# A two-layer Mamba, attention and quantised-FFN kernel: every engine's order rewritten, and 162 products of the identity added on TensorE

## The chip, the core and the metric

The kernel runs on one core of a Trainium2 chip. The metric is the device time of one execution in microseconds (us), lower is better. Before the change it is 393.94 us, the median of three runs (392.65 to 394.93).

TensorE (PE in the profile) multiplies, VectorE (DVE), ScalarE (ACT) and GpSimd (POOL) do the elementwise work, and the SyncE queue (SP) issues most transfers. Each engine runs its own list of instructions in order; between engines there are only semaphores.

## The reference, cut to what matters

Sixteen sequences of 128 tokens (`x`) pass through three blocks, all in float32 (the FFN's weights are rounded to -1, 0, 1 and held as bf16):

```python
x = emb[input_ids]                                    # 16 x 128 x 192
for i in range(2):                                    # two Mamba layers
    xr, res = jnp.split(_rmsnorm(x, norm_w[i]) @ in_proj_w[i], 2, axis=-1)   # 2 x 384 columns
    xr = silu(conv4(xr) + conv_b)                     # causal, 4 taps, by channel
    dt, Bm, Cm = jnp.split(xr @ x_proj_w, [12, 28], axis=-1)
    delta = softplus(dt @ dt_proj_w + dt_proj_b)
    y = selective_scan(xr, delta, A, Bm, Cm, D)       # 16 states by channel
    x = x + y * silu(res) @ out_proj_w
h = x + attention(_layernorm(x))                      # 12 heads of 16; weights relu(1 + s + s*s/2), normalised
out = h + ffn(_layernorm(h))                          # rmsnorm, 8-bit rounding, 192 -> 2 x 512 -> 192
```

## The kernel before, in words

**Tiling.** The Mamba part works on chunks `j` = 0 to 7: layer `j // 4`, group `j % 4` of four sequences (512 columns: `GT`). The 384 channels are `CI` = 3 blocks `c` of 128 partitions. The attention and the FFN work on groups `g` of four sequences and on single sequences `s` = 0 to 15.

**One chunk.** `square_sums`, `raise_squares`, `root_inverse_in` and `scale` normalise; TensorE turns the rows (`turn_in`, line 972, transposes of 128x128), ScalarE takes them out of PSUM (`take_xt`), `project_in` and `project_rest` (lines 983, 989, 991) multiply by the input weights; `first_tap` (ACT) and nine `convolve` (DVE, line 2239) make the convolution; `silu_input`, `silu_gate_in` the activations; `project_x`, `take_xp` and `project_steps` (line 1005) lead to the steps; `magnitude`, `exponential`, `one_plus`, `error` (line 2231), `logarithm`, `rest` (POOL) and `delta` (line 2248) are the softplus. `spread_b` and `spread_cg` (lines 1010 to 1018) spread B and C over the partitions. `input_times_b` (2263), `scan_first` (2269), `memoryless_states` (2277), `skip` (2282), `times_c` (2288) and on POOL `add_first` (1856) and `gate` (1850) make the gated output, `project_out` (1065) projects it in two halves, and `add_h` (2335) adds it to `h`.

**The other states.** State 0 is scanned; for the other 15 a flag (`count_short`, `raise_flag`) tells whether they decay within one step. `states_pe`, `states_dve`, `states_act` load that flag and branch; with these inputs the branch around the loops is taken in all eight chunks.

**Attention and FFN.** `variances`, `root_inverse`, `normalise` (2360) and `turn_x` (1074) start the attention of a group; `project_qk`, `project_v`, then by sequence `scores` (1115), `square_scores` (ACT, 480), `values` (1127), `turn_sums` (1135 and 1138), `divide`, `turn_attention`, `project`. `scores(s)` waits until ScalarE has squared all of `s - 1`. The FFN of a sequence: `turn_input`, two `project_up` (1167), `silu_gate`, `hidden` (2439), `gain` (POOL, 1890), `square_hidden`, `hidden_root`, `hidden_step`, `round_hidden` (2453), `turn_hidden` (1174), `take_hidden` (534), `project_down` (1181), `add_ffn` (2459), and the store of the sequence.

**What sets the order.** Each engine's program is a written-out list of such calls, laid out beforehand by a planner with costs of its own. PSUM has eight banks of 512 columns; the tables `T_BANKS` to `UP_BANKS` give each product its bank, and bare `pe.wait_ge(...)` lines between the calls of TensorE's list wait until the bank's last reader is through. The lists of the four engines must fit each other: whatever stands at the head of a list and waits holds up all behind it.

**`keep_clock`** (line 965) is defined in the kernel before and called nowhere in it: `n` products of the 128x128 float32 identity with itself into bank `b`, with no semaphore; nothing reads the result.

## Time and profile before

| | |
|---|---|
| median of three runs | 393.94 us (392.65 to 394.93) |
| the profiled execution's own time | 396.22 us |
| its span, first to last instruction | 394.2 us |
| TensorE busy | 325.8 us (83%) |
| VectorE busy | 294.0 us (75%) |
| ScalarE busy | 272.4 us (69%) |
| GpSimd busy | 235.3 us (60%) |
| mean granted TensorE clock | 0.908 |

Busy time says how long an engine had something in work. [...] A float32 product appears as two records, a transpose as one.

### The profile page before, as it was taken

To read this page: it belongs to the slowest core of one execution; us is meant where nothing else is said; L and a number is where in the kernel's file an instruction comes from. 1 tells how busy PE (TensorE), PEld (TensorE's weight loads), DVE (VectorE), ACT (ScalarE), POOL (GpSimd) and SP (SyncE) were. 2 spreads that over 40 slices of the span, in tenths; PEclk is the share of its full clock that TensorE was granted. 3 is DMA by queue.
4 is the path that set the end of the run, shared out by engine and by line. 5 is a ranking of instruction groups with operands and counts; after the bars stand their busy time and mean duration, and the time that the engine had idled before them with its cause. 6 is when DMAs were issued, how large, how long until landed. Compare 5 with 4: busy or idle time off the path is not lost. (4 is left out here: it accounts for less than half of the span.)

```text
span 394.2 us, 6391 instructions
## 1 busy us (share of the span) xinstructions
PE 325.8 (83%) x1794; PEld 188.7 (48%) x1794; DVE 294.0 (75%) x636; ACT 272.4 (69%) x552; POOL 235.3 (60%) x316
## 2 busy tenths in 40 slices
PE   0199965768978899998989889988998899899955
PEld 0143422254425534364335558646765646477633
DVE  3019999899899899999998959941365737467874
ACT  2459999696688998799876964353555547566852
POOL 6751168578819459296392691760134836678893
PEclk9999995959899998998979969998999969899976
DMA  6891000000000000000000000000000000000111
GB/s 151 150 274 23 1 2 0 2 1 0 2 1 1 2 0 2 2 1 0 2 1 0 1 3 2 0 2 2 0 2 2 0 2 1 2 12 10 32 60 50
DMA packets 7134, 7.87 MB, mean 20 GB/s; under 512 B 1643, under 2 KB 6138, under 8 KB 7098
## 3 DMA queue, kind: packets, MB, share of 16 engines
q1 hardware_dynamic: 5464, 5.71, 4.9%
q0 software_dynamic: 768, 1.57, 2.8%
q8 instruction: 15, 0.25, 0.2%
q10 hardware_dynamic: 866, 0.17, 0.2%
q14 instruction: 21, 0.17, 0.2%
HBM read 5.87 MB, written 1.57 MB: 19 GB/s over the span
## 5 line engine op out<-in xcount | busy, mean ns | idle before, releaser
L983 PE MATMUL bank<-ring,win 128*128 128x512 f32 x96 | 53.4, 690 | 7.4 <-DVE dmin L2248 3.3
L1856 POOL TENSOR_TENSOR arena<-arena 128x512 f32<-128x512 f32 x24 | 34.0, 1428 | 39.9 <-DVE arena L2282 25.9
L2239 DVE SCALAR_TENSOR_TENSOR pair<-bank,cw,pair 128x508 f32<-128x508 f32 (+2 forms) x72 | 49.8, 733 | 5.8 <-issue 4.7
L1838 POOL TENSOR_TENSOR arena<-arena,dl 128x512 f32<-128x512 f32 x24 | 31.9, 1332 | 22.9 <-DVE dl L2231 22.6
L1065 PE MATMUL bank<-wout,pair 128*128 128x192 f32 x192 | 37.7, 352 | 3.3 <-ACT ring L382 3.3
L480 ACT ACTIVATE du<-bank 128x512 f32<-128x512 f32 x48 | 25.3, 597 | 19.9 <-PE bank L1115 17.4
L1065 PEld LDWEIGHTS bank<-wout,pair 128*128 128x128 f32 x192 | 34.1, 206 | 9.5 <-ACT ring L382 3.7
L1844 POOL TENSOR_TENSOR du<-dl,pair 128x512 f32<-128x512 f32 x24 | 33.1, 1383 | 8.8 <-DVE dmin L2248 8.8
L983 PEld LDWEIGHTS bank<-ring,win 128*128 128x128 f32 x96 | 19.0, 216 | 35.0 <-issue 18.8
L2269 DVE TENSOR_TENSOR_SCAN arena<-arena 128x512 f32<-128x512 f32 x24 | 34.8, 1461 | 0.3
L972 PE MATMUL bank<-ident,ring 128*128 128x128 f32 x64 | 11.7, 330 | 23.8 <-ACT ring L409 19.0
L1850 POOL TENSOR_TENSOR pair<-pair,arena 128x512 f32<-128x512 f32 x24 | 31.2, 1316 | 0.0
L989 PE MATMUL bank<-ring,win_rest 64*128 64x512 f32 x48 | 26.3, 641 | 0.0
L991 PE MATMUL bank<-ring,win_rest 64*128 64x512 f32 x48 | 26.3, 641 | 0.0
L998 PE MATMUL bank<-pair,wx 128*125 128x512 f32 x48 | 24.0, 639 | 1.3 <-issue 1.3
L972 PEld LDWEIGHTS bank<-ident,ring 128*128 128x128 f32 x64 | 8.9, 170 | 30.1 <-issue 23.5
L1890 POOL TENSOR_TENSOR pair<-pair,gout 128x512 f32<-128x512 f32 x16 | 20.5, 1285 | 1.8 <-PE bank L1174 1.1
L335 ACT ACTIVATE pair<-bank,cb,cw 128x512 f32<-128x512 f32 x24 | 18.5, 787 | 3.8 <-PE bank L991 2.3
L1833 POOL TENSOR_TENSOR rstd<-ms,neg_half 128x4 f32<-128x4 f32 x8 | 9.2, 1147 | 19.7 <-DVE ms L2219 16.5
L1167 PE MATMUL bank<-wq,arena 96*128 96x512 bf16 x64 | 18.6, 397 | 1.4 <-ACT arena L507 1.4
L2263 DVE TENSOR_TENSOR arena<-du,bank 128x512 f32<-128x512 f32 x24 | 16.2, 681 | 4.3 <-PE bank L1010 2.8
L2277 DVE TENSOR_TENSOR arena<-du,bank 128x512 f32<-128x512 f32 x24 | 16.3, 678 | 4.1 <-POOL pair L1850 3.5
(177 smaller groups left out, 887.1 us busy)
## 6 DMA issues: line engine op xcount, KB each, us to landing
out<-h SPq DMA_DIRECT2D x16, 96.0 KB, 1.6
win<-in_w SPq DMA_DIRECT2D x2, 384.0 KB
arena<-ffn_in_t SPq DMA_DIRECT2D x1, 768.0 KB
wout<-out_w SPq DMA_DIRECT2D x2, 288.0 KB
win_rest<-in_w SPq DMA_DIRECT2D x2, 192.0 KB
arena<-ffn_out_t SPq DMA_DIRECT2D x1, 384.0 KB
wa<-w_qkv SPq DMA_DIRECT2D x1, 384.0 KB
h<-emb,idx POOLq DMA_INDIRECT x16
```

The costliest lines, as they stand in the source:

```text
L480: nc.scalar.activation(sq[s % 2][:, r, :, :], bank[:, SC_BANKS[s][r], :].rearrange("p (j n) -> p j n", j=JH), ACT.Square, scale=HD ** -0.5 ...
L983: nc.tensor.matmul(bank[:, IN_BANKS[j][m], :], win[:, j // NG, m * P:(m + 1) * P], xtr[:, j % 2, i, :], start=True, stop=False)
L989: nc.tensor.matmul(bank[:, IN_BANKS[j][2 * q], :], rest[64:P, :], xtr[64:P, j % 2, 1, :], start=False, stop=True).then_inc(x_ready if 2 * ...
L991: nc.tensor.matmul(bank[:, IN_BANKS[j][2 * q + 1], :], rest[0:64, :], xtr[0:64, j % 2, 0, :], start=False, stop=True).then_inc(x_ready if ...
L998: last = nc.tensor.matmul(bank[0:XM, XP_BANKS[j], :], wx[:, j // NG, c, :], xc[:, j % NG, c, :], start=(c == 0), stop=(c == CI - 1))
L1065: last = nc.tensor.matmul(bank[:, O_BANKS[j][b], i * D:(i + 1) * D], xc[:, j % NG, c, t0:t0 + LEN], wout[:, j // NG, c, :], start=(c == 0) ...
L1838: nc.gpsimd.tensor_tensor(relu_s[:, c, :], relu_s[:, c, :], dl[:, j % NG, c, :], ALU.subtract).then_inc(rest_done, 1)
L1844: nc.gpsimd.tensor_tensor(du[:, g, c, :], dl[:, g, c, :], xc[:, g, c, :], ALU.mult).then_inc(du_ready, 1)
L1850: nc.gpsimd.tensor_tensor(xc[:, j % NG, c, :], sz[:, j % NG, c, :], yv[:, c, :], ALU.mult).then_inc(gated, 1)
L1856: nc.gpsimd.tensor_tensor(yv[:, c, :], yv[:, c, :], bx[:, c, :], ALU.add).then_inc(yv_done, 1)
L2239: nc.vector.scalar_tensor_tensor(acc, seqs(bank[:, IN_BANKS[j][c], :])[:, :, 0:LEN - tap], cw[:, j // NG, c, TAPS - 1 - tap:TAPS - tap], a ...
L2269: nc.vector.tensor_tensor_scan(bx[:, c, :], da[:, c, :], bx[:, c, :], 0.0, ALU.mult, ALU.add).then_inc(scan_done, 1)
```

## The change

Three things are changed. (1) The order of calls on TensorE, VectorE, ScalarE and GpSimd is new; the planner now charges for long idle times of TensorE. (2) The bank tables, and with them the bare waits on TensorE, are new. (3) 23 calls of `keep_clock`, 162 products together, stand in TensorE's list. Every other call is there as often as before, except one `silus()` and one `exponentials_and_logarithms()` more on ScalarE (each loads an activation table), which a set of gates in chunk 4 now needs. Line numbers of the changed kernel are 2 to 3 higher on TensorE's part (969 is the identity product, 1068 is `project_out`, 1177 `turn_hidden`, 1184 `project_down`) and 37 higher on VectorE's.

```diff
-T_BANKS = ((0, 1), (4, 5), (0, 5), (1, 0), (5, 5), (2, 2), (0, 1), (7, 6))
+T_BANKS = ((0, 1), (4, 5), (4, 5), (2, 2), (0, 3), (1, 5), (0, 1), (6, 0))
...
             turn_in(0, 0)
             turn_in(0, 1)
+            keep_clock(7, 2)
             pe.wait_ge(xt_ready, 2)
             project_in(0, 0)
...
+            states_pe(0)
+            pe.wait_ge(bx_ready, 1)
+            pe.wait_ge(bx_ready, 2)
+            pe.wait_ge(bx_ready, 3)
+            keep_clock(10, 7)
             pe.wait_ge(delta_ready, 4)
+            project_in(2, 2)
+            pe.wait_ge(flag_ready, 1)
+            turn_in(3, 1)
+            project_rest(2, 2)
...
             project_steps(2)
+            pe.wait_ge(delta_ready, 6)
+            keep_clock(29, 5)
             pe.wait_ge(dbl_ready, 3)
             pe.wait_ge(bc_ready, 3)
-            turn_in(3, 1)
-            pe.wait_ge(xt_ready, 8)
             project_out(0, 0)
```

The 23 calls by their `n`, in the order of TensorE's list: 7 (ahead of `project_in(0, 0)`), 1, 1, 3, 4, 10 (behind `states_pe(0)`), 29 (ahead of `project_out(0, 0)`), 1, 1, 7, 8, 4, 9, 2, 3, 7, 16 (between `project_rest(7, 0)` and `project_in(7, 1)`), 6 (ahead of `project_steps(7)`); then none until the last sequences: 5 and 12 around `project_up(14, ...)`, 4 ahead of `project_up(15, 1)`, 6 ahead of `project_down(11)`, 16 ahead of `turn_hidden(12)`.

**TensorE, chunks 1 and 2.** Here stands, before the change, TensorE's list from `project_steps(2)` (line 1005) over half of `turn_in(3, ...)` (972) to `project_out(0, ...)` (1065):

```order
L1005 MATMUL bank<-dbl,wdt 128x512 x3
L972 MATMUL bank<-ident,ring 128x128 x4
L1065 MATMUL bank<-wout,pair 128x192 x12
L983 MATMUL bank<-ring,win 128x512 x2
L1056 MATMUL bank<-shortest,ones 128x1
```

And the same place of the change, from the ten products behind `states_pe(0)` on:

```order
L969 MATMUL bank<-ident 128x128 x10
L985 MATMUL bank<-ring,win 128x512 x2
L974 MATMUL bank<-ident,ring 128x128 x4
L991 MATMUL bank<-ring,win_rest 128x512
L993 MATMUL bank<-ring,win_rest 128x512
L1012 MATMUL bank<-dbl,picked 128x512
L1000 MATMUL bank<-pair,wx 125x512 x3
L1018 MATMUL bank<-dbl,picked 128x512
L1020 MATMUL bank<-bc,not_first 128x512
L1007 MATMUL bank<-dbl,wdt 128x512 x3
L969 MATMUL bank<-ident 128x128 x29
L1068 MATMUL bank<-wout,pair 128x192 x12
```

`project_in(2, 2)` and `turn_in(3, 1)` have moved behind the branch of chunk 0, ten identity products stand before them, and 29 between `project_steps(2)` and `project_out(0, ...)`.

**VectorE, chunks 6 and 7.** The first attention group needs four `normalise` (line 2360, 2397 in the change). Before, this stands around the last three of them; 2239 is `convolve` of chunk 7, 2231 `error(6, ...)`, 2248 `delta(6, ...)`:

```order
L2248 ISA dl,dmin<-bank,arena 128x512
L2248 ISA dmin 128x1
L2231 SCALAR_TENSOR_TENSOR dl<-bank,dl 128x512
L2239 SCALAR_TENSOR_TENSOR pair<-bank,cw,pair 128x4x127 x2
L2231 SCALAR_TENSOR_TENSOR dl<-bank,dl 128x512
L2239 SCALAR_TENSOR_TENSOR pair<-bank,cw,pair 128x4x126 x2
L2239 SCALAR_TENSOR_TENSOR pair<-bank,cw,pair 128x4x125 x2
L2360 TENSOR_SCALAR ring<-h,mv,rstd 128x192 x3
```

In the change, with the flag of chunk 5 (2365), a scan (2306), `times_c` (2325), `delta` (2285), `skip` (2319) and the branch on the flag (2330):

```order
L2365 TENSOR_SCALAR flag<-bank 1x1
L2306 SCALAR_TENSOR_TENSOR arena<-arena 128x512
L2397 TENSOR_SCALAR ring<-h,mv,rstd 128x192
L2325 TENSOR_TENSOR arena<-arena,bank 128x512
L2285 ISA dl,dmin<-bank,arena 128x512
L2285 ISA dmin 128x1
L2319 SCALAR_TENSOR_TENSOR arena<-pair,dskip,arena 128x512
L2397 TENSOR_SCALAR ring<-h,mv,rstd 128x192
L2285 ISA dl,dmin<-bank,arena 128x512
L2285 ISA dmin 128x1
L2276 SCALAR_TENSOR_TENSOR pair<-bank,cw,pair 128x4x127
L2330 TENSOR_LOAD flag
```

All nine convolutions of chunk 7, the last `error` of chunk 6 and the branch on the flag now stand behind the last of the four `normalise`; before, six of the nine, that `error` and the branch stood ahead of it.

**TensorE, the end of the list.** Before, from `project_up(15, ...)` (1167) on; 1174 is `turn_hidden`, 1181 `project_down`:

```order
L1167 MATMUL bank<-wq,arena 128x512 x4
L1181 MATMUL bank<-wq,arena 128x192 x4
L1174 MATMUL bank<-ident,pair 128x128 x4
L1181 MATMUL bank<-wq,arena 128x192 x4
L1174 MATMUL bank<-ident,pair 128x128 x8
```

The change, from the last `project_up(14, ...)` (1170) on:

```order
L1170 MATMUL bank<-wq,arena 128x512 x2
L969 MATMUL bank<-ident 128x128 x12
L1177 MATMUL bank<-ident,pair 128x128 x4
L1163 MATMUL bank<-ident,ring 96x128 x2
L969 MATMUL bank<-ident 128x128 x4
L1170 MATMUL bank<-wq,arena 128x512 x2
L1184 MATMUL bank<-wq,arena 128x192 x4
L1170 MATMUL bank<-wq,arena 128x512 x2
L1184 MATMUL bank<-wq,arena 128x192 x4
L1177 MATMUL bank<-ident,pair 128x128 x4
L969 MATMUL bank<-ident 128x128 x6
L1184 MATMUL bank<-wq,arena 128x192 x4
```

Here the real products keep nearly their order, and the identity products stand between them; 16 more and two `turn_hidden` follow this piece.

## Rows read from the trace of the kernel before

**Rows 1.** The page: TensorE's granted clock, in tenths, in 40 equal slices.

```profile
PEclk9999995959899998998979969998999969899976
```

**Rows 2.** Windows: us, then busy us of PE, PEld, DVE, ACT, POOL; PEclk.

```profile
40.00:204.00 164.00, 135.29 (x454) 65.44 (x453) 154.99 (x268) 142.35 (x270) 105.28 (x82) 0.89 0.00 1
204.00:245.00 41.00, 38.12 (x266) 23.98 (x264) 33.92 (x67) 27.09 (x50) 23.53 (x18) 0.86 0.01 1
245.00:376.00 131.00, 121.46 (x968) 83.51 (x968) 78.61 (x241) 73.16 (x154) 74.20 (x163) 0.95 0.02 6
376.00:394.20 18.20, 8.96 (x51) 6.28 (x49) 10.30 (x25) 7.01 (x14) 11.66 (x24) 0.69 0.17 54
```

**Rows 3.** Waits: engine, line, releaser: us in total, times, longest.

```profile
PE bank L1115 <- ACT du L480: 10.5, 6, 1.8
```

**Rows 4.** TensorE's timeline at the start: start, us, instruction, idle before.

```profile
17.23 1.94 PE L972 MATMUL bank<-ident,ring 128*128 128x128 f32 x8 [17.23 <-ACT ring L409]
20.00 5.84 PE L983 MATMUL bank<-ring,win 128*128 128x512 f32 x8 [0.82 <-ACT ring L382]
28.62 3.68 PE L983 MATMUL bank<-ring,win 128*128 128x512 f32 x8
```

**Rows 5.** TensorE's timeline: three products with the identity, twice, and what follows.

```profile
274.40 1.48 PE L1138 MATMUL bank<-ident,arena 128*128 128x128 f32 x6
275.68 0.63 PE L1160 MATMUL bank<-ident,ring 128*96 128x128 f32 x2
...
279.14 0.83 PE L1138 MATMUL bank<-ident,arena 128*128 128x128 f32 x6
279.81 0.49 PE L1065 MATMUL bank<-wout,pair 128*128 128x192 f32 x2
```

**Rows 6.** Timeline, all engines, around the branch of chunk 0.

```profile
76.08 0.14 DVE L2328 TENSOR_SCALAR flag<-bank 1x1 int32<-1x1 f32 x1
77.47 4.65 POOL L1850 TENSOR_TENSOR pair<-pair,arena 128x512 f32<-128x512 f32 x3
77.54 0.69 ACT L328 ACTIVATE dbl<-bank,one_rows 125x512 f32<-125x512 f32 x1 [2.21 <-PEq L1025]
77.66 0.69 DVE L2263 TENSOR_TENSOR arena<-du,bank 128x512 f32<-128x512 f32 x1 [1.44 <-POOL arena L1856]
```

**Rows 7.** TensorE's timeline: one half of `project_out`, six products in twelve records.

```profile
265.38 2.22 PE L1065 MATMUL bank<-wout,pair 128*128 128x192 f32 x12
```

**Rows 8.** Groups by line: count, busy us, mean ns.

```profile
L2239 DVE SCALAR_TENSOR_TENSOR pair<-bank,cw,pair 128x508 f32<-128x508 f32 (+2 forms) x72 | 49.8, 733 | 5.8 <-issue 4.7 <-ACT pair L335 0.6
L2269 DVE TENSOR_TENSOR_SCAN arena<-arena 128x512 f32<-128x512 f32 x24 | 34.8, 1461 | 0.3
L318 ACT ACT_TABLE_LOAD x9 | 11.5, 1283 | 0.6 <-issue 0.5
```

**Rows 9.** Timeline around the first attention group, TensorE and VectorE.

```profile
202.29 2.29 DVE L2360 TENSOR_SCALAR ring<-h,mv,rstd 128x192 f32<-128x192 f32 x3
205.44 1.97 PE L1074 MATMUL bank<-ident,ring 128*128 128x128 f32 x8
```

**Rows 10.** TensorE's timeline: the second of two adjacent score groups.

```profile
341.06 1.40 PE L1115 MATMUL bank<-dl 32*128 32x256 f32 x12 [1.74 <-ACT du L480]
```

**Rows 11.** Timeline of the last 21 us, all engines.

```profile
373.94 1.02 PE L1167 MATMUL bank<-wq,arena 96*128 96x512 bf16 x4 [0.42 <-ACT arena L507]
377.23 1.02 PE L1167 MATMUL bank<-wq,arena 96*128 96x512 bf16 x4 [0.95 <-ACT arena L507]
381.02 0.74 DVE L2439 SCALAR_TENSOR_TENSOR pair<-bank,deq,pair 128x512 f32<-128x512 f32 x1
383.33 1.27 POOL L1890 TENSOR_TENSOR pair<-pair,gout 128x512 f32<-128x512 f32 x1
386.92 1.09 PE L1174 MATMUL bank<-ident,pair 128*128 128x128 f32 x4 [2.03 <-DVE pair L2453]
391.77 0.42 DVE L2459 SCALAR_TENSOR_TENSOR h<-bank,deq,h 128x192 f32<-128x192 f32 x1 [0.46 <-PE bank L1181]
```

More of the change, by code:

```diff
@@ L1371, in _ @@
-            pe.wait_ge(sz_ready, 18)
-            project_steps(5)
-            pe.wait_ge(sz_ready, 19)
-            project_out(3, 0)
+            pe.wait_ge(xt_ready, 13)
+            pe.wait_ge(conv[1], 18)
+            spread_cg(4)
+            pe.wait_ge(conv[2], 18)
+            pe.wait_ge(xt_ready, 14)
+            project_in(6, 0)
+            pe.wait_ge(sz_ready, 17)
+            project_in(6, 1)
+            project_rest(6, 0)
+            project_rest(6, 1)
+            pe.wait_ge(bx_ready, 15)
@@ L1380, in _ @@
             project_in(6, 2)
+            pe.wait_ge(h_added, 8)
+            spread_b(5)
             pe.wait_ge(conv[0], 21)
[L1382 to L1385 removed]
+            keep_clock(2, 5)
             pe.wait_ge(delta_ready, 16)
@@ L2515, in _ @@
-            times_c(0, 0)
-            scan_first(0, 1)
-            largest_shortfall(0)
-            memoryless_states(0, 2)
-            times_c(0, 1)
-            skip(0, 1)
-            skip(0, 2)
+            input_times_b(0, 2)
+            convolve(2, 2, 1)
+            delta(1, 0)
+            raise_flag(0)
+            scan_first(0, 1)
+            convolve(2, 2, 2)
+            times_c(0, 1)
+            skip(0, 2)
+            convolve(2, 2, 3)
+            error(1, 2)
             scan_first(0, 2)
@@ L2539, in _ @@
-            largest_shortfall(1)
-            scan_first(1, 1)
-            delta(2, 0)
-            add_h(0, 0)
-            add_h(0, 1)
-            times_c(1, 1)
-            memoryless_states(1, 2)
-            input_times_b(1, 2)
-            raise_squares(4)
-            scan_first(1, 2)
-            skip(1, 2)
-            error(2, 2)
-            convolve(3, 0, 1)
-            delta(2, 1)
+            memoryless_states(1, 1)
+            add_h(0, 0)
+            delta(2, 0)
+            input_times_b(1, 1)
@@ new lines, in _ @@
+            input_times_b(1, 2)
+            add_h(0, 1)
+            skip(1, 1)
+            scan_first(1, 1)
+            raise_squares(4)
+            delta(2, 1)
+            memoryless_states(1, 2)
+            error(2, 2)
+            convolve(3, 1, 1)
+            convolve(3, 0, 1)
+            convolve(3, 1, 2)
+            convolve(3, 0, 2)
+            raise_flag(1)
+            convolve(3, 0, 3)
+            delta(2, 2)
+            scan_first(1, 2)
+            largest_shortfall(2)
@@ L2575, in _ @@
-            skip(2, 0)
+            scan_first(2, 2)
+            times_c(2, 1)
+            add_h(1, 0)
+            add_h(1, 1)
             skip(2, 1)
+            skip(2, 2)
+            times_c(2, 2)
             convolve(4, 0, 1)
-            b_times_c(3)
-            memoryless_states(2, 2)
-            scan_first(2, 2)
-            skip(2, 2)
-            times_c(2, 1)
+            error(3, 0)
+            convolve(4, 0, 2)
+            error(3, 1)
+            raise_squares(5)
+            convolve(4, 0, 3)
@@ L2618, in _ @@
-            scan_first(3, 2)
-            raise_squares(6)
-            error(4, 1)
             times_c(3, 1)
@@ L2759, in _ @@
             normalise(4)
             scan_first(7, 1)
+            largest_shortfall(7)
+            memoryless_states(7, 2)
+            times_c(7, 1)
+            add_h(6, 0)
+            skip(7, 1)
+            normalise(5)
+            normalise(6)
             scan_first(7, 2)
-            normalise(5)
-            times_c(7, 1)
-            divide(2)
-            normalise(6)
             normalise(7)
-            skip(7, 0)
-            raise_flag(7)
-            skip(7, 1)
             skip(7, 2)
@@ L2781, in _ @@
             input_gain(1)
-            largest_input(0)
-            variances(2)
-            add_attention(2)
+            round_input(0)
+            take_v(1, 1)
+            largest_input(1)
+            normalise(9)
+            input_inverse(1)
+            add_h(7, 0)
+            add_attention(2)
+            normalise(10)
+            divide(4)
+            normalise(11)
+            add_h(7, 1)
+            round_input(1)
+            add_attention(3)
+            divide(5)
+            add_attention(4)
```

1870 lines of the change are left out of this document (932 added, 938 removed).

## The prediction

> **What bounds the kernel now.** I read the page first, for where the clock falls [rows 1], then windows for who is busy, then waits and timelines of the places that the change touches.
>
> The windows [rows 2] divide the span in three. From 40 to 204 us VectorE works 155.0 of 164 us: the Mamba chunks are bound by VectorE, with ScalarE close behind (142.4). From 204 to 376 us TensorE works 38.1 of 41 and 121.5 of 131 us, while VectorE falls to 78.6 of 131: the attention and the FFN are bound by TensorE, from the moment when `turn_x(0)` opens the attention. The last 18 us are a latency chain (TensorE 9.0 us busy). So two things decide: when `turn_x(0)` comes, and how fast TensorE gets through all that stands behind it.
>
> In the TensorE-bound part 10.5 of its idle us are six waits of at most 1.8 us for ScalarE's squares [rows 3]: two `scores` stand side by side, and the second waits [rows 10]. [...] The last 18.2 us at 0.69 are 11.3 us at half clock.
>
> **The price of an identity product.** Three `turn_sums` products with the identity, six records, take 275.68 - 274.40 = 1.28 us to the next start at the low clock and 279.81 - 279.14 = 0.67 us at the high one [rows 5]: 0.43 and 0.22 us each. A `keep_clock` product has the same shapes and type, so 162 are 36 us of TensorE at the high clock and 69 us at the low one. Since nothing waits for them, they cost only what they overrun of the gap in which they stand; since the queue is in order, all of that falls on the next real product.
>
> **Part A, the first seven.** They stand between the transposes (end 19.17) and `project_in(0, 0)` (20.00), a gap of 0.82 us [rows 4], at the low clock: 7 x 0.43 = 3.0 us, 2.2 us too much. Against it: `project_in`'s first eight records took 5.84 us where the next eight took 3.68 [rows 4], so the clock rose within them. If the seven bring the rise forward to the time when they end, the eight are done at about 19.17 + 2.5 + 3.7 = 25.4 instead of 25.8; if it stays where it was, at 26.7. I take +0.1 us, bounds -0.7 and +0.9.
>
> **Part B, `turn_x(0)`.** Its inputs are the four `normalise`; before, the last three end at 204.58 and `turn_x(0)` starts at 205.44 [rows 9]. In the change six convolutions (0.733 us each [rows 8]), one `error` (an elementwise pass of this size is 0.69 us [rows 6]) and a branch no longer stand ahead of the last `normalise`. A branch costs an engine some 1.3 us: the flag is written at 76.22, and ScalarE, which waited for it, begins at 77.54 [rows 6]. That is 4.40 + 0.69 + 1.3 = 6.4 us off VectorE's path to it. TensorE's own path from the same flag is then longer than VectorE's: four products of 0.92 (3.68 / 4 [rows 4]), the branch, one `project_rest` of 0.95 come to 5.9 us, against 1.46 + 0.69 x 2 + 0.75 + 0.38 x 2 = 4.4 us. So 1.5 us come back, and with the 0.86 us by which TensorE is late now, `turn_x(0)` starts some 5.8 us earlier.
>
> But `project_rest(7, 2)`, `spread_b(6)` and `spread_cg(6)` now stand behind it: 0.95 and some 2.0 us, and six identity products 1.3 us, together 4.2 us more in the TensorE-bound part. **B: -1.6 us.** The bounds: 0 if VectorE has no room to be earlier, -5.8 if the moved products fall into waits.
>
> **Part C, chunks 0 and 1.** Take as zero the writing of chunk 0's flag. VectorE has 1.46 x 2 + 0.73 x 2 + 0.78 + four passes of 0.68 and a branch of 1.3, together 9.2 us, before it asks for `delta(1, 1)`. (The nine are `scan_first` twice, two convolutions, `skip`, `error`, `times_c` twice and `input_times_b`.) TensorE: branch 1.3, ten identity products 2.2, `project_in(2, 2)` 1.8, `turn_in(3, 1)` 0.5: 5.8. ScalarE takes that out (0.7), then two `silu_input`, two `silu_gate_in`, a table load of 1.28 [rows 8] and `logarithm(1, 1)`: 10.8 us. Without the ten, ScalarE would be there at 8.8, ahead of VectorE; they cost 1.6 us.
>
> Next, `logarithm(1, 2)`, `take_xp(2)` and `project_steps(2)` end at 13.2. The 29 products run to 13.2 + 6.5 = 19.7, and the six products of `project_out(0, 0)`, 2.2 us [rows 7], to 21.9. VectorE is through `delta(1, 2)` at 12.3, has a scan, a `skip` and six passes of 0.69 before `add_h(0, 0)`, comes to it at 18.9 and waits 3.0 us. Without the 29, `project_out` could start at 13.2 as well: its last gate ends at 82.12, 5.9 us behind the flag's time of 76.22 now [rows 6], and the same 5.9 us behind `times_c(0, 2)` (7.2) are 13.1. The two groups thus cost 4.6 us of VectorE in the part that VectorE bounds. On the other side, the place is now at half clock (the two slices of 0.5 from 59 to 69 and from 79 to 89 us [rows 1]) and VectorE waits there 1.44 us for a POOL addition [rows 6], which the change moves forward, and some 1.2 us for slow products. I expect all 2.6 us to go. **C: +2.0 us**, bounds -2.6 and +13 (below). The other groups ahead of chunk 7 stand where TensorE already waits for VectorE or ScalarE, so I cost them at nothing; that cover is the 28.7 us by which TensorE is idle in 164 [rows 2].
>
> **Part D, the clock behind `turn_x(0)`.** The three groups of 3, 7 and 16 stand before the place at which the clock is low now (201 to 209 us). I expect it high there: 3.4 us of low clock behind 205.44 give back 1.7 us. [...] The new order has as many adjacent `scores` as the old, six. I give the charge for idle time a fifth, -2.0 us. **D: -3.7 us**, bounds +3 and -12.
>
> [...]
>
> **Part E, the end.** 21 products (5, 12, 4) are 4.7 us, and the waits at that place now are 0.42 and 0.95 us [rows 11]; 3.3 us are too many. `hidden(15)` ends at 381.76 and its `gain` starts at 383.33 [rows 11], so 1.6 us are hidden and 1.7 us come through. The 16 ahead of `turn_hidden(12)`, 3.6 us, come up against a wait of 2.03 us, but the four `take_hidden` and the rest behind them end at about 391.9, by 392.2 now. The half clock there costs the last TensorE pieces some 1.3 us, `turn_hidden` 1.09 us at 386.92 [rows 11] against 0.60 at the high clock. **E: +0.4 us**, bounds -2 and +4.
>
> The extra pair of table loads, 2 x 1.28 us [rows 8], lies on ScalarE, which has 21.6 us free in 164 [rows 2]: 0, or +2.6 if not covered.
>
> **The sum:** 0.1 - 1.6 + 2.0 - 3.7 + 0.4 = -2.8 us. The profiled execution took 396.22 us (span 394.2), and would take 393.4; it is 0.6% above the median, to which I refer: 393.94 - 2.8 = **391.1 us**. Of a difference to the median some 0.5%, 2.0 us, is what a measurement of this kernel can tell from no change.
>
> **The rivals.**
>
> *The low clock meets the identity products (slower).* If the clock is low when the group of 29 starts, it takes 29 x 0.43 = 12.5 us and `project_out(0, 0)` 2.9: VectorE waits 28.5 - 18.9 = 9.6 us instead of 3.0, and the ten cost 2.1 us more, together +8.7: 399.8 us. It decides as soon as the products overrun the gate's time (13.2 us behind the flag) by more than 3.6 us, since VectorE asks 5.8 us behind the gate and `project_out` takes 2.2. For it: the place is at half clock now [rows 1]. Against it: ten and 29 dense products should themselves raise the clock, as eight records did at the start [rows 4]. Chance 0.28.
>
> *The clock stays high in attention and FFN (much faster).* [...] For it: the charge aims at that. Against: the same adjacent `scores`. Chance 0.18.
>
> *The moves cancel.* VectorE's work is the same 294 us; what is put behind the `normalise` is missing later, and TensorE waits for chunk 7's gates. B and D become zero except for the 1.7 us: 394.5 us with C and E. Chance 0.22.
>
> **How the numbers follow.** My forecast has 0.32. It is under 392 in two thirds of its width (388.5 to 394), so faster: 0.18 + 0.20 + 0.06 = 0.44; within 0.5%: 0.11 + 0.13 = 0.24; slower: 0.28 and the rest, 0.32. The range, 384 to 400, reaches to both outer rivals and leaves out the further bounds of C and D.
>
> **What would show it.** Right: the four `normalise` end near 200 us; no low clock between 57 and 89 us, nor between 376 and 390; a wait of VectorE's `add_h` for `project_out(0, 0)` of about 3 us; the identity products at 0.22 us; low clock still beside adjacent `scores`. Wrong: `add_h` does not wait, so the gap was larger than I read; a granted clock of 1.00 throughout 204 to 376; or a new long wait of VectorE in chunks 3 to 6, where I compared the orders only by what stands ahead of the attention.

## The result: slower by 3%, and the profile after

The changed kernel takes 405.97 us (median of 4 runs, 404.57 to 408.46), the kernel before beside it 393.84 us. The ratio is 1.032, 95% interval 1.026 to 1.037. I had said 391.1 us, in a range of 384 to 400. Executions of one kernel differ by up to 11 us here, and the ratios leave out those more than 1.5% above the fastest of their kernel, two strays of 804.7 and 1050.8 us among them.

The page after, with the row of [rows 1] in its new form. VectorE's share fell, TensorE's rose, the granted clock is high at the end (a 9, 90% or more, in each of the last eight slices):

```profile
span 404.0 us, 7039 instructions
PE 352.1 (87%) x2118; PEld 223.5 (55%) x2118; DVE 292.2 (72%) x636; ACT 275.2 (68%) x554; POOL 234.0 (58%) x316
PEclk9999975799999699899999979998899899999999
```

The record of the granted clock has two levels in every trace here, 1.00 (high) and 0.50 (low). The kernel before has 73 of its 394.2 us at 0.50, the changed one 51 of 404.0. At 0.50 an identity product took 0.42 us, at 1.00 it took 0.23 us (the groups of ten and 29 below). The record begins at 24.4 us in the kernel before and at 21.85 us in the changed one; for the time ahead of it there are only the lengths of the products.

The 324 records of the 162 identity products, from the groups by line (busy us, mean ns of one, idle time ahead). They took 45.6 us, 0.28 us each, between my prices of 0.22 and 0.43:

```profile
L969 PE MATMUL bank<-ident 128*128 128x128 f32 x324 | 45.6, 298 | 4.5 <-issue 4.5
```

The stages that the prediction spoke of, cut at `turn_x(0)` and at the end of the last `project_up`. The columns are the window, its length, busy us of TensorE, its weight loads, VectorE, ScalarE and POOL, then the granted clock. Of the kernel before:

```profile
40.00:205.44 165.44, 136.73 (x456) 65.44 (x454) 156.43 (x270) 142.83 (x270) 106.72 (x83) 0.89 0.00 1
205.44:378.20 172.76, 159.39 (x1235) 107.84 (x1234) 112.56 (x309) 101.54 (x209) 98.33 (x183) 0.93 0.02 5
378.20:391.73 13.53, 7.71 (x45) 5.92 (x44) 8.41 (x21) 5.24 (x10) 9.63 (x21) 0.62 0.19 58
```

Of the changed kernel:

```profile
40.00:209.99 169.99, 152.55 (x654) 87.64 (x653) 149.86 (x265) 140.01 (x264) 102.46 (x80) 0.91 0.00 1
209.99:391.10 181.11, 167.25 (x1302) 114.70 (x1301) 118.52 (x316) 108.10 (x218) 105.12 (x192) 0.94 0.02 5
391.10:401.48 10.38, 9.57 (x88) 8.70 (x86) 7.05 (x18) 3.94 (x7) 5.82 (x15) 1.00 0.22 68
```

`turn_x(0)` starts at 209.99 us instead of 205.44 (I had it near 201.7), the stretch to the last `project_up` is 8.4 us longer, the last one 3.1 us shorter: +9.8 us of span. VectorE has 6.6 us less to do ahead of `turn_x(0)`, where I had counted 5.1 us of passes and a branch, and yet the stage is 4.6 us longer: it is idle for 20.1 us instead of 9.0. The rows around chunk 0's branch show for what (engine, line, what it wrote from what, and in brackets the idle time and what ended it):

```profile
72.94 4.15 PE L969 MATMUL bank<-ident 128*128 128x128 f32 x20 [2.33 <-issue]
76.93 1.88 PE L985 MATMUL bank<-ring,win 128*128 128x512 f32 x4
78.64 0.60 PE L974 MATMUL bank<-ident,ring 128*128 128x128 f32 x4
79.28 0.69 ACT L382 ACTIVATE ring<-bank,nw 128x512 f32<-128x512 f32 x1 [4.38 <-PE bank L974]
80.23 1.12 PE L1012 MATMUL bank<-dbl,picked 16*128 16x512 f32 x2
81.39 0.69 DVE L2300 TENSOR_TENSOR arena<-du,bank 128x512 f32<-128x512 f32 x1 [3.80 <-PE bank L1012]
84.02 0.69 DVE L2285 CUSTOM_DVE_ANT_0 dl<-bank,arena 128x512 f32<-128x512 f32 x1 [1.94 <-ACT bank L364]
86.17 6.74 PE L969 MATMUL bank<-ident 128*128 128x128 f32 x58
94.90 0.55 DVE L2372 TENSOR_TENSOR h<-h,bank 128x384 f32<-128x384 f32 x1 [3.08 <-PE bank L1068]
```

The group of ten meets the low clock (0.50 over 72.9 to 76.4 us), 0.42 us each. `project_in(2, 2)` (L985), `turn_in(3, 1)` (L974) and ScalarE's `take_xt` (L382) follow it in the queue, and only then `spread_b(1)` (L1012), for which VectorE's `input_times_b(1, 0)` waits 3.8 us. The group of 29 (58 records at 86.17) runs at the high clock (1.00 over 86.1 to 92.6 us), 0.23 us each, and `add_h(0, 0)` waits 3.1 us, as forecast.

### The profile page after: what moved, and what is told of

Same layout as the page of the kernel before. It is cut to its first block, busy times and chain, and to the rows that moved or that the text cites. A ratio compares the mean times of both kernels' runs of the same rounds, so it can differ in the third digit from the quotient of the medians.

```text
span 404.0 us, 7039 instructions
## 1 busy us (share of the span) xinstructions
PE 352.1 (87%) x2118; PEld 223.5 (55%) x2118; DVE 292.2 (72%) x636; ACT 275.2 (68%) x554; POOL 234.0 (58%) x316
## 4 chain that ended last, share of the span: by engine, by line
PE 59%; ACT 13%; issue 12%; DVE 11%; POOL 3%; DMA 0%; ACTq 0%; DVEq 0%; POOLq 0%
PE bank L969 10%; PE bank L1118 5%; PE bank L985 4%; PE bank L1000 4%; PE bank L1130 3%; PE bank L1068 3%; PE bank L1170 3%; PE bank L1087 3%; PE bank L1138 2%; PE bank L1141 2%; PE bank L991 2%; PE bank L1156 2%; PE bank L1007 2%; ACT du L480 2%; DVE pair L2276 2%
## 5 line engine op out<-in xcount | busy, mean ns | idle before, releaser
L969 PEld LDWEIGHTS bank<-ident 128*128 128x128 f32 x324 | 43.0, 211 | 12.5 <-issue 10.6
L969 PE MATMUL bank<-ident 128*128 128x128 f32 x324 | 45.6, 298 | 4.5 <-issue 4.5
L985 PE MATMUL bank<-ring,win 128*128 128x512 f32 x96 | 47.2, 623 | 2.4 <-DVE h L2372 0.9
L1068 PEld LDWEIGHTS bank<-wout,pair 128*128 128x128 f32 x192 | 32.3, 196 | 5.2 <-issue 3.2
L1068 PE MATMUL bank<-wout,pair 128*128 128x192 f32 x192 | 34.9, 337 | 0.1
L480 ACT ACTIVATE du<-bank 128x512 f32<-128x512 f32 x48 | 25.3, 597 | 13.6 <-PE bank L1118 10.4
L2306 DVE TENSOR_TENSOR_SCAN arena<-arena 128x512 f32<-128x512 f32 x24 | 30.5, 1276 | 1.7 <-ACT arena L390 1.7
L974 PE MATMUL bank<-ident,ring 128*128 128x128 f32 x64 | 11.0, 322 | 22.8 <-ACT ring L409 18.7
L985 PEld LDWEIGHTS bank<-ring,win 128*128 128x128 f32 x96 | 17.5, 197 | 23.9 <-issue 16.5
L1887 POOL TENSOR_TENSOR pair<-pair,arena 128x512 f32<-128x512 f32 x24 | 30.2, 1272 | 0.0
L974 PEld LDWEIGHTS bank<-ident,ring 128*128 128x128 f32 x64 | 8.9, 166 | 29.5 <-issue 20.2
L2314 DVE TENSOR_TENSOR arena<-du,bank 128x512 f32<-128x512 f32 x24 | 16.2, 676 | 6.3 <-PE bank L1020 6.3
L2268 DVE SCALAR_TENSOR_TENSOR dl<-bank,dl 128x512 f32<-128x512 f32 x24 | 16.2, 684 | 5.0 <-ACT bank L359 4.9
```

Source lines behind the costliest of these rows:

```text
L480: nc.scalar.activation(sq[s % 2][:, r, :, :], bank[:, SC_BANKS[s][r], :].rearrange("p (j n) -> p j n", j=JH), ACT.Square, scale=HD ** -0.5 ...
L969: nc.tensor.matmul(bank[:, b, 0:P], ident[:, :], ident[:, :], start=True, stop=True)
L985: nc.tensor.matmul(bank[:, IN_BANKS[j][m], :], win[:, j // NG, m * P:(m + 1) * P], xtr[:, j % 2, i, :], start=True, stop=False)
L1068: last = nc.tensor.matmul(bank[:, O_BANKS[j][b], i * D:(i + 1) * D], xc[:, j % NG, c, t0:t0 + LEN], wout[:, j // NG, c, :], start=(c == 0) ...
L1887: nc.gpsimd.tensor_tensor(xc[:, j % NG, c, :], sz[:, j % NG, c, :], yv[:, c, :], ALU.mult).then_inc(gated, 1)
L2306: nc.vector.tensor_tensor_scan(bx[:, c, :], da[:, c, :], bx[:, c, :], 0.0, ALU.mult, ALU.add).then_inc(scan_done, 1)
```

## The experiments

The kernel before was run beside each; its medians were 393.3 to 394.3 us. Where an edit says that a group is left out, only unread products go. The runs were taken in several sets, so two medians of different sets compare to about 1 us at best; the ratios to the kernel before are the safer measure. Each trace is of one execution, which need not be the median one; where it is not, its time is given.

**1. The order alone, and three parts of the products.** All 162 out; only the groups of 10 and 29 out; only the last 43 out; only the 62 between chunk 2 and `project_steps(7)` out. The edit of the second; the others are of the same kind, with all 23 calls, the last five, and nine.

```diff
-            keep_clock(10, 7)
...
-            keep_clock(29, 5)
```

> All 162 identity products are left out of the changed kernel; orders and banks stay. Theory 1 (the products cost): they are 36 us of TensorE at the high clock, and the three places where TensorE has no gap (the start, chunks 0 and 1, the last 30 us) give back 14 us or more: about 392 us, no slower than the kernel before. Theory 2 (the new order is slower by itself): the time stays at 400 us or above. Rival inside theory 1: without the products the clock falls more, the mean clock goes back to about 0.91, and only half of the 14 us comes back: about 399 us.

Measured 402.38 us (400.4 to 406.8), ratio 1.018 (1.013 to 1.023); the profiled execution took 406.0 us. Theory 2: two thirds of the loss, 8.1 of 12.1 us, is the new order by itself. Theory 1 as I put it, that the order alone is no slower than before, is out.

> Only the groups of 10 and 29 products in chunks 0 and 1 are left out. In the changed kernel VectorE waits 4.2 us for ScalarE, 3.8 us for spread_b(1) and 3.1 us for project_out(0, 0) there. Theory 1: these two groups cost 6 to 8 us: 398 to 400 us, and the add_h wait of 3.1 us is gone. Theory 2: VectorE catches up by turn_x(0) anyway, within 2 us of 406. Rival: without them TensorE stays at the low clock past 77 us, and the slow project_out takes the gain: 403 or more.

Measured 402.08 us, ratio 1.019 (1.015 to 1.024). These 39 products cost 3.9 us (4.8 by the ratios), and without them the other 123 are worth nothing, for good or ill, against the order alone. It is less than theory 1 said and more than theory 2.

> Only the 43 products among the last FFN sequences are left out. They last 9.6 us of TensorE in the changed kernel, in a stretch where it is busy 19.6 of 24 us. Theory 1: they stand on TensorE's path: 5 to 9 us come back, 397 to 401 us, though the clock falls again at the end and costs 1 to 2 us. Theory 2 (the chain at the end goes by VectorE and ScalarE, as I predicted for all but 0.4 us): within 1.5 us of 406.

Measured 407.37 us (403.7 to 412.2), ratio 1.036 (1.030 to 1.041), not below the changed kernel. The 43 products cost nothing that can be measured here: theory 2 holds. The windows after `turn_x(0)` are of the fastest of its six executions (403.7 us; the other five took 406.8 to 412.2), so they show the stretches and not the median. Without the products the last stretch is at 0.83 and TensorE idle for 3.6 us of it, and it is as short as with them, 10.3 and 10.4 us; in that stretch the products filled waits:

```profile
208.20:388.90 180.70, 164.17 (x1260) 111.19 (x1259) 119.36 (x315) 108.19 (x218) 104.69 (x191) 0.93 0.02 5
388.90:399.20 10.30, 6.68 (x44) 5.27 (x42) 7.13 (x21) 4.05 (x7) 6.33 (x15) 0.83 0.25 76
```

> Only the 62 products between chunk 2 and project_steps(7) are left out (groups of 7, 8, 4, 9, 2, 3, 7, 16, 6), which I costed at nothing but for the last six. Theory 1: they stand in gaps, the last six give 1.3 us back: 403.5 to 406. Rival: they overrun too, and 4 us or more come back: 402 or less. Rival: the clock falls without them ahead of turn_x(0) and the time rises to 407 or more.

Measured 404.11 us (399.4 to 410.2), ratio 1.016 (1.010 to 1.023). The scatter of 11 us covers all three; inconclusive beyond "not much".

**2. One move undone in the order alone.**

```diff
             count_short(0)
-            states_pe(0)
             pe.wait_ge(bx_ready, 1)
...
             project_in(2, 2)
+            states_pe(0)
```

> The new order without any identity product, and one move undone: project_in(2, 2) stands ahead of TensorE's branch of chunk 0 again, as in the kernel before, instead of behind it. In the new order alone it starts 2 us behind the flag at the low clock, project_rest(2, 2), turn_in(3, 1) and spread_b(1) stand behind it, and VectorE waits 3.1 us for spread_b(1). Theory 1 (the new order of chunks 0 and 1 put work behind the branch that TensorE had idle time for): spread_b(1) comes some 2 us earlier, VectorE's wait for it falls to about 1 us, and the time is 1 to 2 us under the order alone (402.4 us), near 401. Theory 2 (ScalarE's chain behind the branch is what sets it, because spread_b(1) waits for take_xt through a shared bank): the wait stays near 3 us and the time stays.

Measured 401.84 us (396.8 to 403.0), ratio 1.022 (1.016 to 1.028). The wait did fall to 0.7 us, and in the profiled execution `turn_x(0)` came at 201.2 us instead of 207.9; but that execution took 397.7 us, one of two under 400 among six. The medians do not tell; experiment 6 takes it up on a base with less scatter.

**3. Products ahead of the first transposes of the kernel before.**

```diff
+            keep_clock(30, 7)
             turn_in(0, 0)
```

> The kernel before, with 30 identity products ahead of the first transposes, where TensorE is idle until 17.2 us. Theory 1: the rise of the clock depends on how long TensorE has been working, so the transposes take 1.1 us instead of 1.9 and the first project_in group 3.7 instead of 5.8 us: 3.0 us less, 391 us. Rival: the next thing behind it is a transfer or ScalarE's scaling of the next rows (17 us of loads still run until 35 us), and less than 1 us reaches the end: 393.5. Rival: the products still run when the rows are ready, and it is slower: 396 or more.

Measured 397.96 us, ratio 1.010 (1.005 to 1.016): slower, by a way that I had not listed. The clock was high for the transposes (recorded at 1.00 from 12.7 us on; 1.10 us instead of 1.94), but ScalarE, with the rows ready at 18.1 us, began to take them out at 21.7, released by nothing on an engine ("remote"). TensorE stood idle for 5.0 us, the clock fell again (0.50 from 19.5 to 26.4 us), and `project_in` took 5.30 us, not the 3.68 of its next group, which ran at 1.00:

```profile
6.86 9.72 PE L971 MATMUL bank<-ident 128*128 128x128 f32 x60 [6.86 <-DVE weakest L2190]
16.99 1.10 PE L976 MATMUL bank<-ident,ring 128*128 128x128 f32 x8 [0.41 <-ACT ring L409]
21.71 1.26 ACT L382 ACTIVATE ring<-bank,nw 128x512 f32<-128x512 f32 x2 [4.77 <-remote]
23.07 5.30 PE L987 MATMUL bank<-ring,win 128*128 128x512 f32 x8 [4.98 <-ACT ring L382]
```

**4. Products in the waits between adjacent `scores` of the kernel before**, the waits of [rows 3, 10], and both edits together.

```diff
+            keep_clock(7, SC_BANKS[1][0])     # and for 5, 7, 9, 11, 13
             scores(1)
```

> The kernel before, with 7 identity products (1.5 us at the high clock) ahead of the second of each of the six adjacent scores pairs, where TensorE waits 1.74 us for the squares. Theory 1 (these waits are what lets the clock fall): the low clock between 205 and 378 us, 23.9 us now, falls to 8 us or less, and 8 us come back: 386 us. Rival (the fall has another cause, or the products make no difference to it): the low clock stays near 24 us, the time within 2 us of before, 393 to 396. Rival (the waits are not really idle, or the clock is low there): each group overruns by 1.5 us, and it is slower by 3 us or more.

Measured 389.12 us (388.7 to 389.6), ratio 0.989 (0.983 to 0.994): faster than both kernels. Theory 1 in the main, with half of the 8 us that it gave: the clock over the stretch behind `turn_x(0)` goes from 0.93 to 0.98, and only two low stretches are left in it, 6.6 us. The product group stands where the wait was:

```profile
204.80:370.20 165.40, 161.46 (x1318) 114.15 (x1318) 112.26 (x308) 100.88 (x207) 98.09 (x181) 0.98 0.02 5
261.50 1.83 PE L971 MATMUL bank<-ident 128*128 128x128 f32 x14
263.32 1.14 PE L1119 MATMUL bank<-dl 32*128 32x256 f32 x12
```

> Both of the two edits at once on the kernel before: 30 products ahead of the first transposes and 7 in each of the six waits between adjacent scores. If both theories hold, the gains add up: 383 us. If only one does, it takes that one's time; a sum larger than the parts would say that the two act through the same clock.

Measured 392.9 us, ratio 0.997 (0.993 to 1.001): the two add within 1 us, -4 and +5.

The control, the same 42 products ahead of the first of each pair, so that the wait stays:

```diff
+            keep_clock(7, SC_BANKS[0][0])     # and for 4, 6, 8, 10, 12
             scores(0)
```

> Control for the six groups of 7: the kernel before, with the same 42 products ahead of the first of each pair, where TensorE does not wait for squares. Theory (what counts is that the wait of 1.74 us is filled): 6 x 1.5 = 9 us of products fall on TensorE's path, the clock falls as before: 399 to 403 us. Rival (more work anywhere holds the clock): some 5 of the 9 us come back: 396 to 398. Second rival (the wait that follows is shortened by as much, since the squares are late by the clock and not by TensorE): near 394.

Measured 411.39 us (405.4 to 412.8), ratio 1.040 (1.031 to 1.048), twice the price of the products. The wait of 1.8 us is still there, behind the products, and the clock over the stretch is 0.91, the lowest of all runs:

```profile
224.83 1.80 PE L971 MATMUL bank<-ident 128*128 128x128 f32 x14
226.56 1.14 PE L1119 MATMUL bank<-pair 32*128 32x256 f32 x12
229.52 1.75 PE L1119 MATMUL bank<-pair 32*128 32x256 f32 x12 [1.82 <-ACT du L480]
204.40:392.90 188.50, 175.27 (x1318) 122.34 (x1318) 114.27 (x310) 101.33 (x209) 98.97 (x183) 0.91 0.02 4
```

What counts is the place: the same 42 products in the wait gain 4 us and 1.1 us ahead of it lose 18. That they worsened the clock I had not expected. In the profile (an execution of 411.7 us) a low stretch of the clock begins within 2 us of the end of five of the six waits, and within 2 us of four of the six in the kernel before; why one more, and longer ones (35.7 us of low clock in the stretch instead of 23.7), no run shows.

**5. The same six groups in the new order**: once in the kernel without the groups of 10 and 29, once in the order alone (in both for `scores` 2, 5, 7, 9, 11, 13).

> The changed kernel without the groups of 10 and 29, with 7 identity products ahead of the second of each of its six adjacent scores pairs. Theory (the waits between adjacent scores let the clock fall, in the new order as in the old): the low clock behind turn_x(0), 20.5 us in the run without them, falls to 8 us or less, and 4 to 6 us come back: 397 us. Rival: in the new order the low clock has other causes too, and it stays within 1.5 us of 402.

Measured 395.0 us (391.5 to 397.8), ratio 1.004 (1.000 to 1.008): 7 us less than without them (6 by the ratios). The theory holds.

> The new order without any of its 162 products, with 7 in each of the six waits between adjacent scores: against the kernel before with the same six groups (389.1 us) the two differ by the order alone, at a high clock behind turn_x(0) in both. Theory 1 (the new order costs what it costs through its sequence, 2.5 us of later turn_x(0) and some 4 us more work behind it): 6 to 8 us above, 395 to 397. Theory 2 (the new order lost by a lower clock): the difference shrinks to 2 us or less, 391.

Measured 391.14 us (389.3 to 391.8), ratio 0.992 (0.989 to 0.995): 11.2 us less than the order alone (10.3 by the ratios), and only 2.0 us over the kernel before with the same groups (1.3 by the ratios, whose intervals overlap). Theory 2, with one reservation: the clock behind `turn_x(0)` is not the same in both, 1.00 here and 0.98 there. The clock behind `turn_x(0)` of the order alone, and with the groups:

```profile
207.90:390.80 182.90, 165.25 (x1247) 110.31 (x1246) 119.64 (x316) 108.00 (x218) 104.80 (x192) 0.93 0.02 5
206.60:377.20 170.60, 163.36 (x1332) 112.26 (x1331) 119.82 (x316) 107.91 (x218) 105.38 (x193) 1.00 0.02 5
```

**6. On that base (391.1 us): the move undone, the groups put back.** Edits as in 1 and 2.

> On the quieter base of the new order with the six groups of 7 (391.1 us): project_in(2, 2) ahead of TensorE's branch of chunk 0, the one move undone. In the earlier profile it took VectorE's wait for spread_b(1) from 3.1 to 0.7 us, but the medians (401.8 and 402.4) did not tell. Theory 1 (that place is a part of what the new order loses before turn_x(0)): 1 to 2.5 us less, 389 to 390, turn_x(0) at 204 to 205.5 us instead of 206.6. Theory 2 (VectorE meets another wait later): within 0.7 us of 391.1 and turn_x(0) near 206.6.

Measured 388.82 us (387.0 to 392.5), ratio 0.988 (0.983 to 0.992). The interval overlaps that of the base, so 2.3 us is a possible size and not a sure one. `turn_x(0)` comes at 203.4 and, in the last run of this group, at 200.0 us, instead of 206.6, and VectorE's wait for `spread_b(1)` is 0.8 instead of 3.0 us. But the profiled execution with 203.4 took 392.5 us, longer than the base's 391.3: behind `turn_x(0)` its clock is low for 9.1 us, where the base has none. Of the base and of this kernel:

```profile
71.25 3.75 PE L985 MATMUL bank<-ring,win 128*128 128x512 f32 x4 [2.63 <-issue]
77.46 1.12 PE L1012 MATMUL bank<-dbl,picked 16*128 16x512 f32 x2
78.62 0.69 DVE L2283 TENSOR_TENSOR arena<-du,bank 128x512 f32<-128x512 f32 x1 [3.02 <-PE bank L1012]
```

```profile
69.07 3.36 PE L985 MATMUL bank<-ring,win 128*128 128x512 f32 x4 [1.09 <-DVE dmin L2268]
73.86 1.12 PE L1012 MATMUL bank<-dbl,picked 16*128 16x512 f32 x2
75.72 0.69 DVE L2283 TENSOR_TENSOR arena<-du,bank 128x512 f32<-128x512 f32 x1 [0.75 <-PE bank L1012]
```

> The same base with only the groups of 10 and 29 products put back in their places. Theory 1 (they delay VectorE's chain in chunks 0 and 1 by what was measured on the changed kernel, 3.9 us): 394 to 396. Theory 2 (most of that is caught up by turn_x(0)): 392 or less. I had put their cost at 4.6 us.

Measured 395.62 us (394.6 to 396.7), ratio 1.005 (1.002 to 1.007): +4.5 us. The size is theory 1's and my 4.6, the way is only in part. `add_h(0, 0)` waits 3.1 us, and VectorE's waits from 58 to 100 us are 9.9 us instead of 5.1; but `turn_x(0)` starts at 206.7, 0.1 us from the base: what was lost is made up by then. From 40 us to `turn_x(0)` the clock is low for 37.5 us instead of 51.2, which may be how. In the profiled execution the difference arises behind it, where the clock is low for 6.8 us (231 to 238) and was not in the base. In the 10 us ahead of that TensorE was busy for 9.75 us, with no wait over 0.5 us. Why the clock fell there, no run shows.

> The same base with only the 43 products of the last sequences put back. Without the six groups of 7 they cost nothing (407.4 without, 406.0 with them), since what they cost came back through the clock. Theory 1 (they pay for themselves only where the clock would otherwise be low; here it is high already up to 380 us): they now cost 2 to 4 us, 393 to 395. Theory 2 (they lie in waits): within 0.7 us of 391.1.

Measured 392.68 us (390.8 to 394.2), ratio 0.996 (0.993 to 0.998): +1.5 us (the intervals overlap). The direction is theory 1's, the size less.

> The best of the new order: the six groups of 7, project_in(2, 2) ahead of the branch, and the seven products at the start, which brought the first project_rest 0.35 us forward in the changed kernel. If the parts add up: 0.4 us under the run with the moved project_in alone, near 389. Rival: nothing that can be measured.

Measured 389.94 us (387.0 to 393.7), ratio 0.992 (0.989 to 0.995): the seven at the start add nothing that can be measured.

**7. A try at the best.** The kernel before with the six groups, the seven at the start, and

```diff
+            keep_clock(10, 3)
             pe.wait_ge(yt_ready, 12)
             project_down(11)
...
+            keep_clock(8, 3)
             pe.wait_ge(y_done, 16)
             turn_hidden(14)
```

> A try at a kernel that beats both: the kernel before with 7 products in each of the six waits between adjacent scores, the changed kernel's 7 products at the start, and 10 and 8 products in the two waits of 2.4 and 2.0 us near the end, where the clock is low for 10.2 us. Theory: the six groups bring it to 389.1 as measured, the start gives 0.4, and a high clock at the end gives up to 1.3 us: 387.5. Rival: the products at the end meet the low clock and overrun, 390 or more.

Measured 387.98 us (386.9 to 389.6), ratio 0.988 (0.982 to 0.993), the lowest median of all. The clock at the end is 1.00 instead of 0.62, and that stretch is still 14.0 us long:

```profile
369.10:383.10 14.00, 9.23 (x80) 8.04 (x80) 8.24 (x22) 5.14 (x9) 9.52 (x21) 1.00 0.19 57
```

The median is 1.1 us under that of the six groups alone, the ratio 0.1% under it, with intervals that overlap: the start and the high clock at the end together are worth 1 us at most. TensorE waits there for VectorE and ScalarE.

**What the profiles say side by side.** All in us, of the one profiled execution of each kernel, the low clock from the trace's record of what was granted: VectorE's waits from 58 to 100 us, the time at the low clock from 40 us to `turn_x(0)`, the start of `turn_x(0)`, the low clock from there to the last `project_up`, the time from `turn_x(0)` to the end of the span, and the execution's own time.

| kernel | waits | low ahead | `turn_x(0)` | low behind | behind | time |
|---|---|---|---|---|---|---|
| before | 2.6 | 37.7 | 205.4 | 23.7 | 188.8 | 396.2 |
| changed | 12.2 | 30.7 | 210.0 | 20.5 | 194.0 | 406.0 |
| changed, without 10 and 29 | 7.1 | 30.7 | 207.6 | 20.5 | 195.6 | 405.1 |
| order alone | 5.2 | 51.2 | 207.9 | 27.3 | 196.1 | 406.0 |
| order alone, move undone | 2.7 | 37.5 | 201.2 | 26.7 | 194.6 | 397.7 |
| order, six groups | 5.1 | 51.2 | 206.6 | 0.0 | 182.7 | 391.3 |
| the same, move undone | 2.5 | 41.0 | 203.4 | 9.1 | 187.1 | 392.5 |
| the same, 10 and 29 back instead | 9.9 | 37.5 | 206.7 | 6.8 | 186.0 | 394.8 |
| before, six groups | 2.6 | 34.3 | 204.8 | 6.6 | 181.9 | 388.7 |

Single executions differ: the run without the last 43 products, whose list is that of the changed kernel until then, had 9.1 us of waits and not 12.2, and 17.1 us of low clock ahead and not 30.7.

## Why the prediction was wrong, point by point

**How the miss adds up.** Against the profiled execution I had expected 393.4 us and it took 406.0: 12.6 us more. Of these, 8.3 arose by `turn_x(0)` (209.99 instead of some 201.7), which is mostly part C: VectorE's waits there grew by 9.6 us, where its sum had +2.0; 4.3 arose behind it, where B, D and E together gave +0.9 us and the time from `turn_x(0)` to the end grew from 188.8 to 194.0, by 5.2.

**Part A: right.** The first `project_rest` starts at 25.42 us, 0.35 us sooner; I had said +0.1, bounds -0.7 and +0.9. The seven took 0.42 us each, and `project_in`'s first eight records 3.60 us instead of 5.84; the record of the clock begins at 21.85 us, with 1.00, where it began at 24.4 before:

```profile
18.93 3.12 PE L969 MATMUL bank<-ident 128*128 128x128 f32 x14
21.89 3.60 PE L985 MATMUL bank<-ring,win 128*128 128x512 f32 x8
```

**Part B: the gain ahead was there and did not arrive; the work behind was undersized.** I said `turn_x(0)` would start "some 5.8 us earlier". VectorE's path was shortened; but in the changed kernel and in the order alone `turn_x(0)` came 4.6 and 2.5 us later. With `project_in(2, 2)` ahead of the branch it came at 201.2, 203.4 and 200.0 us in three profiles. The first of them has the waits (2.7 and 2.6 us) and the low clock (37.5 and 37.7 us) of the kernel before, and its `turn_x(0)` is 4.3 us earlier than there: so much of the 5.8 us existed. The order alone does not show it, and the difference begins in chunk 0, in part C: the move undone took away 2.5 us of VectorE's waits and, with them, 10 to 14 us of low clock ahead of `turn_x(0)`, and the runs do not part the two.

The work behind `turn_x(0)`: I costed 2.95 us for the three moved steps. Compared at nearly the same clock (the order with the six groups against the kernel before with them) TensorE is busy for 163.4 instead of 161.5 us. Taking off (1 - clock) x busy, 0 and 3.2 us, my estimate of what the low clock adds (at 0.50 a product took twice as long, 0.43 instead of 0.22 us [rows 5]), leaves 5 us more, with an error of 1 us since the clock has two decimals. That part was undersized by some 2 us.

**Part C: the failed step.** I wrote that VectorE has nine passes and a branch, "together 9.2 us, before it asks for `delta(1, 1)`". One of the nine is `input_times_b(1, 0)`, the first behind the branch, and it needs `spread_b(1)`. In the new order that stands behind the branch, the ten products, `project_in(2, 2)`, `turn_in(3, 1)` and a wait for ScalarE's `take_xt`, since it takes the bank that `turn_in(3, 1)` has just filled. I laid TensorE's queue out to `logarithm(1, 1)` and never asked it for `spread_b(1)`: a wait of 3.8 us. I also costed the queue at the high clock and expected "all 2.6 to go" of the waits there; the clock was low from 56 to 76 us, the ten took 4.15 us and not 2.2. VectorE's waits from 58 to 100 us are 3.8, 3.1, 2.2, 1.9 and 1.2 us, 12.2 where they were 2.6 and where I had left 4.6. The order alone has 5.2 us of them, which I had put at nothing, 3.1 of it for `spread_b(1)`; with `project_in(2, 2)` ahead of the branch again they are 2.7.

The group of 29 did what I said: 6.74 us long (6.5) and a wait of 3.1 us (3.0). That the two groups cost 4.6 us was borne out in size, by the medians (3.9 and 4.5 us) and by VectorE's waits (5.1 and 4.8 us more with them). But the waits alone do not make the time: on the base of experiment 6 they were made up ahead of `turn_x(0)`, where the clock was also low for 13.7 us less. Two slips of arithmetic changed nothing: ScalarE without the ten is there at 8.6, not 8.8, and the sum of the third rival is 394.6, not 394.5.

**Part D: the sum was near, the reasoning not.** Over the two stretches behind `turn_x(0)` (to 391.73 and 401.48 us), (1 - clock) x busy goes from 11.2 + 2.9 to 10.0 + 0 us: 4.1 us back, where I had 3.7. But 2.9 of it is the last stretch, and that is held high by the last 43 products (1.00 with them, 0.83 without). In the middle one the low clock falls from 23.7 to 20.5 us, and that is the 3.4 us at `turn_x(0)` which the groups of 3, 7 and 16 were to remove: 1.7 us back, as forecast. No run shows the 2.0 us that I took for the charge, a fifth of what I thought the low clock there to cost: the order alone is at 0.93 there, as before, and its clock is low for 27.3 us where the kernel before has 23.7. My bound of -12 us and the 384 us at which the range begins were estimates too; the most that a run took back behind `turn_x(0)` was 13.4 us, on the new order with the six waits filled, and 6.9 us on the old. The low clock stayed with the adjacent `scores`, as I read from [rows 10]: four of the five low stretches of the changed kernel begin within 2 us of the end of such a wait; the fifth, at 261 us, does not. What I did not do is draw the conclusion: those six waits, 10.5 us, are the place for the products.

I had counted the six waits as 10.5 us of idle time and left what they do to the clock out of the sum, since each is short. That was wrong. Filling six waits of 1.74 us took the clock of that stretch from 0.93 to 0.98 on the old order and to 1.00 on the new, so waits of 1.74 us matter here. They are not all of it either: with the six waits filled the clock was still low for 6.6, 6.8 and 9.1 us behind `turn_x(0)` in three profiles, twice with no wait of TensorE over 0.5 us just ahead.

**Part E: right in size.** I said +0.4 us, from 37 of the 43 products: the six ahead of `project_down(11)`, 1.3 us, are missing from the sum. Leaving all 43 out changed nothing (407.4 against 406.0 us, with intervals that overlap); with the clock high already, they cost 1.5 us. In the last stretch they lie in waits; that those ahead of it bring back through the clock what they cost is my reading, and no run shows it. Nor is the shorter end their work: from the last `project_up` to the end of the span it is 12.2 to 14.5 us in every kernel of the new order, with them and without, and 16.0 to 16.9 in every kernel of the old.

**The rivals.** The low clock meeting the products was half true: it met the ten and not the 29. Its 399.8 us is still too low, since the order itself lost 8.1 us. No rival of mine had the new order slower by itself by more than a microsecond. Of the signs I named, `add_h`'s wait, the high clock from 376 to 390 us and the low one beside the `scores` came; the low clock from 56 to 76 us and the last `normalise`, which ended at 208.6 us and not near 200, spoke against me.

How much of the 8.1 us is what: with the six waits filled in both, 1 to 2 us is left (391.1 against 389.1 us), and with `project_in(2, 2)` moved the medians are level (388.8 and 389.1); neither difference is clear of the intervals. The other 6 us go with the six waits: filling them gave the new order 10 to 11 us and the old one 4 to 5. The profiles show where the difference comes from. In the new order all of the 27.3 us of low clock in that stretch went, and the time behind `turn_x(0)` fell by 13.4 us; in the old one 17.1 of 23.7 us went, and it fell by 6.9. So the two orders are not level at an equal clock: the new one had the better clock, and some 5 us more TensorE work behind `turn_x(0)`. Why the clock came back wholly in the one and not in the other stays open.

## What to carry to other kernels

- When steps move past a branch, walk VectorE's list from the branch and ask of *each* pass what it reads and where that now stands in TensorE's queue, shared banks included. The sum of an engine's own work is a bound, not a path.
- Unread products were worth their price here inside a wait that TensorE has anyway and that the clock falls after: 7 products in each of six waits of 1.74 us, 389.1 us instead of 393.4. The same products 1.1 us earlier, in front of work, made the kernel some 20 us slower than that (411.4 us).
- A planner's order and its filling should be tested apart: here the order cost 8.1 us and its 162 products 4 more, while 42 products in six waits gained 4 us on the old order.

## What the runs showed of the hardware that was not expected

- While the loads still run, an engine can stand still with nothing on another engine to wait for. In the kernel with both early edits (30 products at the start and the six groups), the products after 16 us came with pauses of 1.1 us between weight loads put down to "issue", and the transposes ended 4 us late. The 30 products thus cost 4 to 5 us in both kernels that had them, once through TensorE and once through ScalarE. From 18 to 20 us the DMA engines were busy all the time (1.06 and 1.03), but so they were in the kernel before (1.05), without such pauses. What the engines stood still for, no run shows.

```profile
17.61 0.30 PEld L971 LDWEIGHTS bank<-ident 128*128 128x128 f32 x2 [1.13 <-issue]
19.03 0.41 PEld L971 LDWEIGHTS bank<-ident 128*128 128x128 f32 x3 [1.12 <-issue]
22.51 0.69 ACT L382 ACTIVATE ring<-bank,nw 128x512 f32<-128x512 f32 x1 [5.51 <-PE bank L976]
```

- Executions of one kernel scatter with the clock that they are granted, and filling the six waits does not always end that: 400.4 to 406.8 us for the order alone, 389.3 to 391.8 with the six groups, but 387.0 to 392.5 with the move undone as well. There the two executions of 392.5 us had a mean granted clock of 0.929 and those of 387.0 and 387.3 us one of 0.942.
- The clock can be low with TensorE busy nearly all the time: with the groups of 10 and 29 put back it was low from 231 to 238 us, and from 221 to 231 us TensorE had been busy for 9.75 us.
